# A transformer block on one core: two row sums a head instead of three, contexts divided inside the attention, the w2 folding moved, and a projection without GpSimd

## The reference, cut to what matters

```python
x = L0_attn_query                                   # [2, 2048, 512], float32
mod = (_silu(c) @ wmod).reshape(2, 6, 1, -1)        # sa, ca, ga, sb, cb, gb
ga, gb = sign(g) * maximum(abs(g), 0.25)            # of both
h = _layernorm(x) * (1 + ca) + sa
mixed = h @ Wqkv.T                                  # 16 heads x (q, k, v) x 32
attn = softmax(q @ k.T / sqrt(32))                  # 32 times [2048, 2048]
out = (attn @ v) @ Wproj.T + bproj
x = x + ga * out
h = _layernorm(x) * (1 + cb) + sb
hidden = fwht(_silu(h @ W1.T) * (h @ W3.T))         # Walsh-Hadamard over 2048
x = x + gb * (hidden @ W2.T)
```

## Time and profile before

| | us |
|---|---|
| median of three runs | 3419.07 |
| lowest and highest | 3417.18, 3424.57 |
| the profiled execution | 3422.99 |
| its span | 3421.2 |
| TensorE busy | 3173.1 (93%) |
| VectorE busy | 1892.1 (55%) |
| GpSimd busy | 1588.4 (46%) |
| ScalarE busy | 1534.8 (45%) |

### The profile page before, as it was taken

The page is one execution under the profiler, slowest core; times in us unless marked ns, Lnnn a source line. Parts: engine busy times, 40 slices in busy tenths (PEclk is TensorE's granted clock), DMA queues, the critical chain, the costliest instruction groups (busy, mean ns, idle before and its releaser), DMA issues. The chain is left out here.

```text
span 3421.2 us, 48695 instructions
## 1 busy us (share of the span) xinstructions
PE 3173.1 (93%) x15340; PEld 2114.3 (62%) x15340; DVE 1892.1 (55%) x3144; ACT 1534.8 (45%) x2869; POOL 1588.4 (46%) x566
## 2 busy tenths in 40 slices
PE   5899799999999999999999998667999999999998
PEld 3688555545555555545555552456888888888887
DVE  5443398778777777777777780653333233223232
ACT  3333146666666666656666665233322222222221
POOL 5000059999888998989989992540000000000000
PEclk7999879999999999999999999878999999999999
DMA  5556537877777777777777763854221121121111
GB/s 213 163 164 183 157 67 166 173 161 163 167 156 168 160 162 157 158 165 162 160 159 163 166 135 76 245 189 164 84 83 47 56 71 44 57 70 44 59 56 34
DMA packets 150990, 446.92 MB, mean 131 GB/s; under 512 B 27398, under 2 KB 45062, under 8 KB 116044
## 3 DMA queue, kind: packets, MB, share of 16 engines
q0 software_dynamic: 28064, 199.24, 28.9%
q1 hardware_dynamic: 122668, 244.39, 24.6%
HBM read 167.78 MB, written 80.23 MB: 72 GB/s over the span
## 5 line engine op out<-in xcount | busy, mean ns | idle before, releaser
L1009 DVE TENSOR_REDUCE mxp<-pmax 128x1 f32<-128x512 f32 x2048 | 1258.9, 681 | 373.3 <-PE pmax L830 372.8
L966 ACT ACTIVATE prob<-pexp 128x512 f32<-128x512 f32 x2048 | 1037.9, 623 | 576.5 <-PE pexp L875 491.0
L830 PE MATMUL pmax<-kst,qst 96*128 96x512 f32 x2048 | 870.7, 433 | 41.4 <-issue 21.0
L1066 POOL TENSOR_TENSOR gsum<-gsum,prob 128x2048 f32<-128x2048 f32 x186 | 877.6, 4718 | 17.9
L875 PE MATMUL pexp<-qst,kst 98*128 98x512 f32 x2048 | 827.9, 424 | 45.2 <-ACT prob L966 45.2
L830 PEld LDWEIGHTS pmax<-kst,qst 96*128 96x128 f32 x2048 | 407.7, 199 | 327.1 <-DVE mxp L1009 184.1
L875 PEld LDWEIGHTS pexp<-qst,kst 98*128 98x128 f32 x2048 | 399.8, 196 | 246.5 <-ACT prob L966 174.3
L1066 POOL TENSOR_TENSOR gsum<-prob 128x2048 f32<-128x2048 f32 x93 | 472.0, 5076 | 76.9 <-ACT prob L966 76.9
L884 PE MATMUL pctx<-prob,v 128*32 128x512 f32 x4096 | 498.2, 603 | 0.0
L1642 DVE TENSOR_TENSOR hid<-sil,pl 128x512 f32<-128x512 f32 x128 | 88.0, 688 | 638.6 <-PE pl L51 631.6
L51 PE MATMUL pg<-h2f,w 128*128 128x512 f32 x1536 | 371.1, 391 | 1.1 <-issue 1.1
(11 more groups left out here) (109 smaller groups left out, 1757.6 us busy)
## 6 DMA issues: line engine op xcount, KB each, us to landing
gsum<-prob POOLq DMA_DIRECT2D x124, 1024.0 KB, 9.7
gsum<-gsum POOLq DMA_DIRECT2D x62, 1024.0 KB, 8.5
w<-w_scratch SPq DMA_DIRECT2D x128, 256.0 KB, 2.6
qst<-q_scratch SPq DMA_DIRECT2D x96, 256.0 KB, 6.4
kst<-k_scratch SPq DMA_DIRECT2D x96, 256.0 KB, 7.2
xin<-in_L_attn_query_dram SPq DMA_DIRECT2D x16, 1024.0 KB, 8.5
q_scratch<-obq SPq DMA_DIRECT2D x32, 512.0 KB, 5.0
k_scratch<-obq SPq DMA_DIRECT2D x32, 512.0 KB, 3.6
```

Source lines behind the costliest of these rows:

```text
L830: pe.matmul(pmax[:, bank, :], qst[0:KR, slot, qt * P:(qt + 1) * P], kst[0:KR, slot, kc * TOK:(kc + 1) * TOK], start=True, stop=True).then_ ...
L966: act.activation(prob[:, kt % RING, j * TOK:(j + 1) * TOK], pexp[:, score_bank(r, n), :], ACT.Exp, scale=SCALE).then_inc(exp_done, 1)
L1009: dve.tensor_reduce(mxp[:, par, u // QJ, u % QJ:u % QJ + 1], pmax[:, bank, :], X, ALU.max).then_inc(mx_done, 1)
L1066: pool.tensor_tensor(dst, a, prob[:, kt % RING, :], ALU.add).then_inc(add_done, 1)
```

## The change

**Preparation.** W2 is not touched any more. Wqkv comes in four loads, Wproj in one, wmod in four without reuse of a buffer, and the low parts are VectorE's, straight from PSUM. GpSimd has nothing to do. The folding of W2 goes into `project_qkv`, a quarter of it (128 rows of W2, all 2048 columns) with each of the tiles 0, 2, 4 and 6: GpSimd loads it and does 8 butterflies of 128x1024, TensorE turns it behind product 9 and multiplies it behind product 11, ScalarE and VectorE read the results.

```diff
+    FOLD_AT = (0, 2, 4, 6)
+    FOLD_TURN, FOLD_MULT = 9, 11
+    STAGES = 4
...
+                def fold_turn(s, b):
+
+                    t = 2 * s + b
+                    n = FOLD_AT.index(t)
+                    pe.wait_ge(h_hi, DC * (t + 2))
+                    pe.wait_ge(h_full, DC * (t + 2))
+                    pe.wait_ge(w2_fly, 2 * STAGES * (n + 1))
+                    for c in range(HC):
+                        last = pe.transpose(pt[:, c // TK, c % TK * P:(c % TK + 1) * P], wn[:, c * P:(c + 1) * P], ident[:, :])
+                        if c % TK == TK - 1:
+                            last.then_inc(w2_turned, 1)
+
+                def fold_mult(s, b):
+
+                    n = FOLD_AT.index(2 * s + b)
+                    pe.wait_ge(keep["had_in"], 16)
+                    for i in range(DC):
+                        pe.wait_ge(w2_taken, DC * n + i + 1)
+                        pe.matmul(pt[:, i, :], had[:, :], wt[:, i * D:(i + 1) * D], start=True, stop=True).then_inc(w2_mm, 1)
...
+            @block.gpsimd
+            def _(pool):
+                def butterfly(n, m):
+
+                    stage, minus = m // 2, m % 2
+                    h = 1 << stage
+                    src, dst = (wt, wn) if stage % 2 else (wn, wt)
+                    src = src[:, :].rearrange("p (n t w) -> p t n w", t=2, w=h * P)
+                    dst = dst[:, :].rearrange("p (n t w) -> p t n w", t=2, w=h * P)
+                    if m:
+                        pool.wait_ge(w2_fly, 2 * STAGES * n + m)
+                    pool.tensor_tensor(dst[:, minus], src[:, 0], src[:, 1],
+                                       ALU.subtract if minus else ALU.add).then_inc(w2_fly, 1)
+
+                for n in range(DC):
+                    if n:
+                        pool.wait_ge(w2_turned, DC * n)
+                    pool.dma_start(wn[:, :], ins["w2"][n * P:(n + 1) * P, :]).then_inc(w2_in, 16)
+                    if n:
+                        pool.wait_ge(w2_scaled, DC * n)
+                        pool.dma_start(scratch["w2"][:, :, (n - 1) * P:n * P].rearrange("c p n -> p c n"),
+                                       wt[:, :].rearrange("p (c n) -> p c n", c=HC)).then_inc(w2_out, 16)
+                        pool.wait_ge(w2_out, 16 * n)
+                    pool.wait_ge(w2_in, 16 * (n + 1))
+                    for m in range(2 * STAGES):
+                        butterfly(n, m)
```

```diff
-ORDER = "MqMqMqMqMqMqqMqM"
-POOLED = ((0, 1, 2, 3), (5, 6, 7, 8), (11, 12, 13, 15))
-CARRIED = (4, 9, 10, 14)
-MERGES = 6
+ORDER = "qM" * 8
+POOLED = ((0, 1, 2, 3, 4), (5, 6, 8, 9, 11))
+CARRIED = (7, 10, 12, 13, 14, 15)
+UNITS = len(POOLED)
 ADDS = sum(len(g) - 1 for g in POOLED)
-TURN_AFTER, UNIT_AFTER = 48, 55
-INVERT_AT = 44
+TURN_AFTER, UNIT_AFTER = 48, 39
+INVERT_AT = 20
...
-                    if exists(g - 1):
-                        if exists(g + 3):
+                    if exists(g + 3):
+                        if exists(g - 1):
                             sp.wait_ge(pv_done, KT * g)
-                            load(g + 3, (r + 3) % SLOTS)
-                        store_ctx(g - 1, par, i * 2 + (r - 1) // 2)
-                    else:
                         load(g + 3, (r + 3) % SLOTS)
                     if exists(g - 2):
-                        fetch_sum(g - 2, r % 2, i * 2 + (r - 2) // 2 + 1)
+                        fetch_sum(g - 2)
+                        spread_rec(g - 2)
+                    if exists(g - 1):
+                        store_sum(g - 1)
                     if exists(g + 1):
                         max_row(g + 1, (r + 1) % SLOTS)
                     if exists(g - 2):
-                        store_rec(g - 2, r % 2)
-                    if exists(g - 1):
-                        store_sum(g - 1, par)
+                        store_ctx(g - 2)
+                    if g == 1:
+                        sp.wait_ge(bias_lo, 1)
+                        sp.dma_start(raw(bias[1:2, :]), raw(blow[:, :])).then_inc(bias_up, 16)
 
                 for g in range(3):
...
-                    pe.wait_ge(merged[5], 16 * (g + 1))
+                def unit(g, k):
+
+                    if k == 0:
+                        if exists(g + 2):
+                            ring_free(g + 1, "unit")
+                        else:
+                            pe.wait_ge(m_split, 2 * HEADS)
+                    pe.wait_ge(merged[LAST_CARRY[k]], 16 * (g + 1))
                     for j in range(QJ):
                         last = pe.matmul(pmax[j * HD:(j + 1) * HD, ring_bank("unit"), :], ones[:, :],
-                                         first_sum(r)[:, j * TOK:(j + 1) * TOK], start=True, stop=True)
+                                         group_sum(k, g)[:, j * TOK:(j + 1) * TOK], start=(k == 0),
+                                         stop=(k == UNITS - 1))
                     last.then_inc(unit_done, 1)
...
+                    before = [n for n in range(i) if CARRY_TO[n] == k]
+                    if before:
+                        pool.wait_ge(merged[before[-1]], 16 * (g + 1))
+                    else:
+                        pool.wait_ge(add_done, ADDS * g + adds_until(POOLED[k][-1]))
+                    pool.dma_start(group_sum(k, g), prob[:, kt % RING, :], accum_op=ALU.add).then_inc(merged[i], 16)
+
+                def divide(g):
+
+                    pool.wait_ge(ctx_read, g + 1)
+                    pool.wait_ge(rec_in, 16 * QJ * (g + 1))
+                    pool.tensor_tensor(ctxo[:, g % OUT, :], ctxo[:, g % OUT, :], recb[:, :], ALU.mult).then_inc(divided, 1)
...
+                    for m in (1, 2, 3, 4):
+                        add(g, 0, m)
+                    carry(g, 0)
+                    add(g, 1, 1)
+                    add(g, 1, 2)
+                    carry(g, 1)
+                    add(g, 1, 3)
+                    add(g, 1, 4)
+                    carry(g, 2)
+                    carry(g, 3)
                     if g >= 2:
-                        pool.wait_ge(unit_done, g - 1)
-                    add(g, first_sum(g), 0, 1)
...
+                        divide(g - 2)
+                    carry(g, 4)
+                    carry(g, 5)
```

```diff
-                    pe.wait_ge(c_hi, DC * (t + 1))
-                    pe.wait_ge(c_lo, DC * (t + 1))
                     for k in range(TK):
                         if t:
                             pe.wait_ge(scaled, TK * t + k + 1 - TK)
-                        split_product(pe, po[:, k, :], lambda a, c: cs[:, t % 2, a, c, k * P:(k + 1) * P],
-                                      lambda a, c: wp[:, a, c, :], range(DC)).then_inc(mm, 1)
+                        for c in range(DC):
+                            if k == 0:
+                                pe.wait_ge(c_hi, DC * t + c + 1)
+                                pe.wait_ge(c_lo, DC * t + c + 1)
+                            split_product(pe, po[:, k, :], lambda a, c: cs[:, t % 2, a, c, k * P:(k + 1) * P],
+                                          lambda a, c: wp[:, a, c, :], (c,), start=(c == 0), stop=False)
+                        pe.matmul(po[:, k, :], ones[:, :], bias[:, :], start=False, stop=True).then_inc(mm, 1)
...
-            @block.gpsimd
-            def _(pool):
-                def scale_ctx(t):
-                    pool.wait_ge(ctx_in[t % 2], 16 * (t // 2 + 1))
-                    pool.wait_ge(rec_in[t % 2], 4 * RECS * (t // 2 + 1))
-                    for c in range(DC):
-                        pool.tensor_tensor(cin[:, t % 2, c, :], cin[:, t % 2, c, :], rb[:, t % 2, c, :],
-                                           ALU.mult).then_inc(c_scaled, 1)
...
                     if t >= 2:
                         act.wait_ge(mm, TK * (t - 1))
+                    act.wait_ge(ctx_in[t % 2], 16 * (t // 2 + 1))
                     for c in range(DC):
-                        act.wait_ge(c_scaled, DC * t + c + 1)
...
                 for t in range(TILES):
+                    if t >= 2:
+                        high_parts(t - 2)
                     if t + 2 < TILES:
                         ctx_high(t + 2)
-                    if t >= 2:
-                        high_parts(t - 2)
```

763 lines of the change are left out of this document (346 added, 417 removed).

## The result

The changed kernel takes 3597.27 us (median of 4 runs, 3595.12 to 3598.36) against 3420.63 (4 runs, 3417.18 to 3424.57): ratio 1.0515, 95% interval 1.0497 to 1.0533. The forecast was 3487, with a range to 3590. The side and the first cause were right; the time lies 7 us outside the range.

The account below looks back on a forecast made before the run. Attention was held bound by GpSimd's chain of additions and serial accumulating DMAs, TensorE 3.9 us below. From 3422.99, -79 for the other stages and +147 for attention gave 3491, less 4: 3487 us; range 3430 to 3530, wider 3325 to 3590.

Parts of the forecast that it names:

- Preparation, -52: Stage before the first product: w2 work leaves, first product near 57 instead of 109.5 us; -52, ends -60 and -40.
- Projection, +21.5: Query/key/value projection: w2 transposes and Hadamard products return to a TensorE without idle time, butterflies hidden on GpSimd; +21.5 us.
- Gap, -10.5: End of attention to first output product: TensorE's idle time falls from 24.50 to about 14 us; -10.5.
- Output projection, -38: Output projection: scaling and small loads go, 186 us becomes 148, between 129 and 167; -38.
- TensorE's floor, 48.8: Attention: TensorE alone needs 48.3 us a head plus 0.5 for the second sum's matmuls, 48.8.
- The inversion: Attention: VectorE's earlier reciprocal waits 7.0 us a head for sums fetched behind the loads; heads of 57.1, +147 us.
- the clock term: Attention: TensorE's stop in each head brings half clock for 6.7 us, costing 3.3.
- GpSimd's chain, 54.3: Attention: GpSimd's additions and two serial chains of carries take 54.3 us a head, from 51.8 to 55.0.
- The two waits lie mostly beside each other: Attention: VectorE's wait for sums and GpSimd's wait for landings overlap, so the larger counts: 57.1 over 54.3 us.
- Rival 3, 3583: Attention: the loads delay the carries by some 6 us, cycle 60.3, 3583 us; chance 0.14.
- The fit for one DMA of the Trainium skill: Carry landings: 2.0 us plus bytes over 436 GB/s, 4.4 us for 1 MB; not used, the trace decided.
- Rival 2: Attention gets no longer, carry 13 landing in 9.7 us gives 51.8 a head, 3328 us; chance 0.14.

Follow-up runs that it names:

- e4_before_attention: Preparation and qkv projection of the changed kernel with attention and output projection of the kernel before: 3373.60 us, 0.9861 of the kernel before.
- e6_small_carries: e1_inv44 with the carries of tiles 12 to 15 moving 512 of 2048 columns, the rest left out of the row sums: 3225.68 us.
- e15_before_inv20: The kernel before with only the reciprocal moved from behind 44 reductions to behind 20: 3547.28 us, 1.0373 of the kernel before.
- e12_small_inv20: e6_small_carries with the reciprocal back behind 20 reductions: 3225.68 us, 0.9416 of the kernel before.
- e14_light_loads: e1_inv44 with q and k rows loading 512 of 2048 columns from head 4 on, so most scores are wrong: 3433.75 us.
- e5_loads_late: e1_inv44 with the seven loads of a head moved behind the sums in SyncE's step: 3449.72 us, 1.0074 of the kernel before.
- e1_inv44: The changed kernel with the reciprocal back behind 44 reductions: 3494.42 us, 1.0211 of the kernel before.
- e8_old_sums: The changed kernel with the row sums of before, reciprocal behind 44 reductions, and contexts divided by VectorE: 3334.15 us, 0.9745 of the kernel before.
- e9 to e11: Tile 15's carry (last run: also 14's) put behind next-head additions, on e5_loads_late, e1_inv44 and e5_loads_late: 3419.44, 3486.48 and 3482.40 us.
- e13_old_sums_join: e8_old_sums with GpSimd's second join moved behind one more carry and one more addition: 3309.14 us, 0.9670 of the kernel before.

## Why the prediction was right in its first cause and too low in its time

The prediction called itself wrong if a head was over 59 us, and it is 60.8. Term by term:

*Preparation, -52:* measured -61, beyond the end of its range by 1. The last modulation step began at 34.65, as the loads' term had it, and the first product came 13.7 later, not the 22 that I had given the chain without a row: one of the two modulation steps and the turn of Wproj were done by then, beside the loads.

*Projection, +21.5:* +21. *Gap, -10.5:* -10. *Output projection, -38:* -45. The working of this term had a slip: 186 less a third of the 85.6 us of waiting is 157 and not 167, and the middle would have been 143, or -43. The stages beside the attention gave -93 where -79 was forecast, within the bounds of -100 to -55. This was luck for the total: with -79 the time would have been 3611. e4_before_attention has the first two alone, -50 at the metric, with heads of 52.0.

*TensorE's floor, 48.8:* 48.4 in e6_small_carries. The term of +0.5 was misread: the eight rows that took 1.07 are one sum's four matmuls (a head now has 16 rows of L944, and had 8 of L896), so the second sum costs 1.07. With 48.4 measured, the 48.3 of before can't have been all TensorE's need; what else it held stays open.

*The inversion:* right as a mechanism, and right in size for the kernel whose rows it was worked out from (e15_before_inv20: 7.6 in the mean against 7.0). In the changed kernel it is 12.2 in the mean, 13.1 in the head shown. The step that failed is "I take the landing of v, in front of which lies one carry as it will after the change". After the change there are two, at S + 3 and S + 10, since both now wait for landings. With them SyncE's issues take 10.1 us, the fetch is issued at S + 15.5 and it lands 11.8 later; e12_small_inv20 and e14_light_loads put 11 us of its lateness on the carries and 3.5 on the loads' bytes. I read the neighbours of the fetch from the old queue although the order rows of the change had moved them. The rest of the prediction's sum holds but for the clock term, as TensorE's restart in the head shown and its granted clock by stretch say:

```profile
1289.73 0.80 PE L877 MATMUL pmax<-kst,qst 96*128 96x512 f32 x1 [10.94 <-DVE mxp L1053]
...
1291.00:1294.00 3.00, 3.00 (x8) 2.32 (x8) 2.88 (x6) 2.15 (x4) 0.01 (x1) 0.50 0.35 87
...
1296.00:1298.00 2.00, 2.00 (x19) 0.77 (x12) 0.54 (x1) 0.04 (x1) 1.73 (x2) 1.00 0.35 70
```

The stop is 10.9, and 13.1 - 2.7 + 0.7 is 11.1. TensorE's rows keep the spacing of half clock until 1294.2, 4.4 us and not 6.7, which costs 2.2 and not 3.3. With the floor of 48.4 that gives 48.4 + 11.1 + 2.2 = 61.7, and this head took 61.7 (context reads at 1266.88 and 1328.54). With the mean wait of 12.2 the same sum gives 60.8, which is the mean head.

*GpSimd's chain, 54.3:* right as a limit (55.7 in e5_loads_late), but it was not the second limit in the changed kernel. The landings of the pair 13 and 15 were 14 and 16.5 us where I had 12.2 for the first, and they act on ScalarE through the ring slot of tile 15: 57.4. The prediction asked what GpSimd's queue waits for and left out what waits for the landing of its last carry. It named the wait for that slot at product 28, but only to say that the sums' matmuls cost nothing beside it, and gave the wait itself no price. With the inversion taken away the heads were 57.4 all the same, so a head near the forecast's 57.1 would not have shown which of the two causes held it.

*"The two waits lie mostly beside each other":* right in kind. Taking away the first (60.8 to 57.4) gave 103 us of the 266 that attention grew; the other 160 go with the new sums, as e1_inv44 against e8_old_sums says.

*Rival 3, 3583:* its time was the nearest, its cause was a part only. e14_light_loads puts the loads' bytes at 2 us a head, 61 us in all, and six to seven remain without them. Its rule of service in turns was not tested by itself: the landings of the loads and of the carries both grew where they met (13.4 for v against 9.4, 16.2 for a carry against 9.7), which fits the packet-by-packet turns of the Trainium skill ("DMA: Bandwidth & Descriptors", section "Queues, rings and completion order"), and a shared limit of bytes as well.

*The fit for one DMA of the Trainium skill* ("DMA: Bandwidth & Descriptors", section "Anatomy of one DMA") would have given the chain no weight. It gives 4.4 us for 1 MB. The carries landed after 7.6 us (the median of 62 in e6_small_carries) to 16.5 (e1_inv44), so it does not hold for these accumulating transfers.

*Rival 2* (attention no longer) is out: head 60.8.

What stays open: why a carry under way makes SyncE's issues longer, and how the 7 us between e14_light_loads and e6_small_carries divide between the bytes of the carries and their serial waits. e9 to e11 moved the waits without taking them away, and a version whose last two carries go to sums of their own was not tried.

## What to carry to other kernels

When a queue of transfers is on the path, price a moved wait with the queue as it will be after the change, all engines' issues in time order about the waiting one, not with the neighbours that it has now. A buffer that a DMA frees is free at the landing: two serial 1 MB accumulations at the end of a period cost two landings under load (14 and 16.5 us here), and the reader of the ring pays it even where the issuing engine has slack. And several parts of one change should be priced against each other's limit: here -93 us of plain gain lay under two losses of 103 and 160, and the old sums with the new stages give 3334 (e8_old_sums), and 3309 with one join moved (e13_old_sums_join).
